# Quantised layer of an eight-stage transformer kernel: weight rounded on GpSimd in quarters, transforms placed in the gaps of the scale chain, products in groups

## What is computed

```python
def _compute_scale(t):
    return FP8_MAX / jnp.maximum(jnp.max(jnp.abs(t)), 1e-12)
def _quantize_fp8(t, scale):
    return jnp.clip(t * scale, -FP8_MAX, FP8_MAX).astype(jnp.float8_e4m3fn)
# third pair, feed-forward: one scale for all of layernorm(x), one for the weight
x_scale, w_scale = _compute_scale(x2), _compute_scale(weight)
out = jnp.matmul(_quantize_fp8(x2, x_scale).astype(f32), _quantize_fp8(weight.T, w_scale).T.astype(f32))
x = x + out * (1.0 / x_scale * (1.0 / w_scale))
# fourth pair, attention: correlation by Fourier transforms of x and of the context
corr = ifft(fft(q) * conj(fft(k))).real      # k and v are the context, so their transforms do not depend on x
```

## Time and profile before

| | |
|---|---|
| median of 3 runs | 1503.25 us (1502.2 to 1504.23) |
| profiled execution, its own time | 1506.02 us |
| its span (first to last instruction) | 1504.3 us |
| busy share PE / DVE / ACT / POOL | 92% / 72% / 51% / 48% |
| mean granted TensorE clock | 0.974 |
| the stage `quantised_ffn` in it | from 1195.05 us to 1235.78 us; the next stage's first matmul starts at 1236.90 us |

### The profile page before, as it was taken

One profiled execution on the slowest core, in us unless ns is written; L12 is line 12 of the kernel. 1 busy time (PEld: TensorE's weight loads), 2 busy tenths in 40 slices (PEclk: granted clock), 3 DMA queues, 4 the chain that ended last, 5 costly groups with the idle time before them and its releaser, 6 DMA issues. The chain is left out here.

```text
span 1504.3 us, 31394 instructions
## 1 busy us (share of the span) xinstructions
PE 1388.1 (92%) x11352; PEld 828.5 (55%) x11352; DVE 1076.6 (72%) x2125; ACT 762.6 (51%) x2476; POOL 723.0 (48%) x748
## 2 busy tenths in 40 slices
PE   5888599998999999888999999999999688889998
PEld 4776244445777777545555555655555235434444
DVE  7998555645666766667989888898877889965212
ACT  4777363222433433347766666666665457655111
POOL 4788552012434433856666666666665405734000
PEclk9999699999999999899999999999999899999999
DMA  7999572225999998757765556756534401646000
GB/s 187 191 174 175 127 182 41 55 39 107 171 180 198 166 153 133 131 134 172 152 146 112 117 114 109 141 112 117 106 73 80 131 3 28 132 84 112 22 7 28
DMA packets 524569, 174.62 MB, mean 116 GB/s; under 512 B 482576, under 2 KB 507600, under 8 KB 524416
## 3 DMA queue, kind: packets, MB, share of 16 engines
q1 hardware_dynamic: 524416, 172.62, 59.3%
HBM read 53.27 MB, written 2.10 MB: 37 GB/s over the span
## 5 line engine op out<-in xcount | busy, mean ns | idle before, releaser
L1887 POOL TENSOR_TENSOR a_q_ss<-a_q_ss,half 128x4 f32<-128x4 f32 x64 | 90.2, 1410 | 167.3 <-DVE a_q_ss L1796 83.8
L1709 ACT ACTIVATE a_probs<-a_masked,a_negmax 128x128 f32<-128x128 f32 x256 | 99.6, 390 | 101.4 <-DVE a_negmax L1767 101.4
L72 PE MATMUL bank<-a_wq_hi,xn_pair 128*128 128x512 f16 (+1 forms) x384 | 140.0, 365 | 8.7 <-DVE a_v_hl L1129 3.8
L1224 POOL TENSOR_TENSOR a_p_hl<-a_probs,a_p_hl 128x512 f16<-128x512 f32 x64 | 74.4, 1163 | 143.3 <-DVE a_p_hl L1145 143.3
L73 PE MATMUL bank<-a_wq_lo,xn_pair 128*128 128x512 f16 (+1 forms) x384 | 139.9, 364 | 0.0
L74 PE MATMUL bank<-a_wq_hi,xn_pair 128*128 128x512 f16 (+1 forms) x384 | 139.7, 364 | 0.0
L72 PE MATMUL bank<-a_wo_hi,a_o_hi 128*128 128x512 f16 x256 | 97.5, 381 | 4.4 <-DVE x_state L1783 3.5
L73 PE MATMUL bank<-a_wo_lo,a_o_hi 128*128 128x512 f16 x256 | 97.4, 380 | 0.0
L74 PE MATMUL bank<-a_wo_hi,a_o_lo 128*128 128x512 f16 x256 | 97.3, 380 | 0.0
L1902 POOL TENSOR_TENSOR a_normal<-a_probs,a_recip 128x512 f32<-128x512 f32 x64 | 90.3, 1410 | 5.0
L652 POOL TENSOR_TENSOR a_p_hl<-a_probs,a_p_hl 128x512 f16<-128x512 f32 x64 | 77.7, 1226 | 25.8 <-DVE a_p_hl L563 17.4
(11 more groups left out here) (472 smaller groups left out, 5017.2 us busy)
## 6 DMA issues: line engine op xcount, KB each, us to landing
a_no<-in_L_xattn_Wo SPq DMA_DIRECT2D x9, 1024.0 KB, 5.8
a_nq<-in_L_xattn_Wq SPq DMA_DIRECT2D x8, 1024.0 KB, 5.8
a_n_wq<-in_L_xattn_Wq SPq DMA_DIRECT2D x4, 768.0 KB, 6.2
a_n_wo<-in_L_xattn_Wo SPq DMA_DIRECT2D x4, 768.0 KB, 6.6
a_nk<-in_L_xattn_Wk SPq DMA_DIRECT2D x9, 256.0 KB, 3.2
a_nv<-in_L_xattn_Wv SPq DMA_DIRECT2D x9, 256.0 KB, 3.8
f_v_hat<-in_L_ffn_w SPq DMA_DIRECT2D x2, 1152.0 KB, 6.8
x_state<-in_x SPq DMA_DIRECT2D x8, 256.0 KB, 4.4
```

What stands on the lines that cost most here:

```text
L72: pe.matmul(out, lh, rh, start=start, stop=False)
L1224: pool.tensor_tensor(p_hl[s % PN][:, 1, t, :], probs[unit(s, t) % PROBS][:, :, :].rearrange("p h n -> p (h n)"), p_hl[s % PN][:, 0, t, :], ...
L1709: m = act.activation(probs[s % 2][:, h, :], src, ACT.Exp, bias=negmax[s % 2][:, h:h + 1], accum_out=total[s % 2][:, h:h + 1])
L1887: pool.tensor_tensor(r[:, :], r[:, :], K.half[:, 0:n], ALU.pow).then_inc(root_done.sem, 1)
```

## The change

- POOL takes over three of the four rounding steps of the weight (`round_weight`), in quarters of 128x512, by four instructions a quarter. DVE keeps the exponent bits (`exponents`), now per quarter, and no longer touches the whole weight.
- The first eight transforms stand between the transposes of the scale chain: one behind the first, two behind the second, one behind the third, four behind the fourth. The tables `spec` and `vspec` are loaded in the stage before, on SP behind the context, into buffers that live longer.
- The columns of the rows have eight buffers (`xq_t`), so ACT no longer waits for products; `tw` is filled three batches ahead.
- The products are done in groups: none before the transposes of batch 4, then 0 and 1; 2; 3 and 4; 5, 6 and 7. DVE's adds follow: 0 after rounding 5; 1 and 2 after 6; 3 after 7; the others among the statistics.

```diff
@@ wide_attention, SP
                     if s == TOTAL:
                         quant.load_context(sp, quant_in)
+                        for name, tile in (("spec", down.spec), ("vspec", down.vspec)):
+                            sp.dma_start(tile[:, :, :], tables[name]).then_inc(tables_in, 16)
                 sp.wait_ge(quant_in, 32)
+                sp.wait_ge(tables_in, 32)
@@ quantised_ffn
-    EARLY, FIRST = 12, 6
-    LATER = {i: list(range(EARLY + 2 * i, EARLY + 2 * i + 2)) if i < 4 else [EARLY + 4 + i] for i in range(B)}
+    AHEAD, RING, LEAD = 2, 3, 8
+    SPREAD = [[0], [1, 2], [3], [4, 5, 6, 7]]
...
+    PRODUCTS = {4: [0, 1], 5: [2], 6: [3, 4], 7: [5, 6, 7]}
+    ADDS = {5: [0], 6: [1, 2], 7: [3]}
...
-        xq_t, ident16 = [sb(f"xq_t{i}", [P, KT, P], BF16) for i in range(2)], sb("ident16", [P, P], BF16)
+        xq_t, ident16 = [sb(f"xq_t{i}", [P, KT, P], BF16) for i in range(B)], sb("ident16", [P, P], BF16)
@@ POOL
+                def round_weight(k):
+                    w, bits = Q.nw[:, k, :], Q.te[:, k, :].bitcast(F32)
+                    pool.wait_ge(w_bits, k + 1)
+                    pool.tensor_scalar(w, w, -Q.FP8_MAX, Q.FP8_MAX, ALU.max, ALU.min).then_inc(w_clipped, 1)
+                    pool.tensor_scalar(bits, bits, 2.0 ** -6, Q.MAGIC, ALU.max, ALU.mult).then_inc(w_magic, 1)
+                    pool.wait_ge(w_clipped, k + 1)
+                    pool.wait_ge(w_magic, k + 1)
+                    pool.tensor_tensor(w, w, bits, ALU.add).then_inc(w_sum, 1)
+                    pool.wait_ge(w_sum, k + 1)
+                    pool.tensor_tensor(wq[:, k, :], w, bits, ALU.subtract).then_inc(w_rounded, 1)
...
+                for k in range(KT):
+                    round_weight(k)
@@ DVE
+                def exponents(k):
+                    dve.wait_ge(w_scaled, k + 1)
+                    dve.tensor_scalar(Q.te[:, k, :], Q.nw[:, k, :].bitcast(I32), 0x7F800000, None, ALU.bitwise_and).then_inc(w_bits, 1)
...
+                for k in range(2):
+                    exponents(k)
                 widen(1)
+                exponents(2)
                 scale(1)
-                bits = Q.te.bitcast(F32)
-                dve.wait_ge(w_scaled, KT)
-                link(dve.tensor_scalar(Q.te, Q.nw.bitcast(I32), 0x7F800000, None, ALU.bitwise_and))
-                link(dve.tensor_scalar(bits, bits, 2.0 ** -6, Q.MAGIC, ALU.max, ALU.mult))
+                exponents(3)
                 round_fp8(0)
-                link(dve.scalar_tensor_tensor(Q.nw, Q.nw, -Q.FP8_MAX, bits, ALU.max, ALU.add))
-                dve.scalar_tensor_tensor(wq[:, :, :], Q.nw, Q.TOP, bits, ALU.min, ALU.subtract).then_inc(w_rounded, 1)
...
@@ PE
+                def product(b):
+                    pe.wait_ge(t_bank.freed(b), t_bank.n_drained(b))
...
+                    y_bank.wait_free(pe, b)
+                    for k in range(KT):
+                        if b == 0:
+                            pe.wait_ge(w_rounded, k + 1)
+                        m = pe.matmul(y_bank[b][:, :], xq_t[b][:, k, :], wq[:, k, :], start=(k == 0), stop=(k == KT - 1))
...
+                for b in batches:
+                    turned(b)
+                    beside(BESIDE[b])
+                    for ready in PRODUCTS.get(b, []):
+                        product(ready)
@@ ACT
+                spectra.copy(act, 0)
                 act.wait_ge(scale_done[0], 1)
                 for k in range(KT):
-                    act.activation(Q.nw[:, k, :], Q.nw[:, k, :], ACT.Copy, scale=Q.scale[:, 0:1]).then_inc(w_scaled, 1)
+                    scale_weight(k)
+                    if k < 3:
+                        spectra.copy(act, k + 1)
                 act.wait_ge(scale_done[1], 1)
...
-                    if b >= 2:
-                        act.wait_ge(y_bank.filled(b - 2), y_bank.n_filled(b - 2))
```

More of the change, by code:

```diff
@@ L2601, in quantised_ffn @@
         spread = K.bank[2:4]
-        w_scaled, w_rounded = K.sem("f2_w_scaled"), K.sem("f2_w_rounded")
+        w_scaled, w_bits, w_clipped, w_magic, w_sum, w_rounded = (
+            K.sem(f"f2_w_{n}") for n in ("scaled", "bits", "clipped", "magic", "sum", "rounded"))
         batches = list(range(B))
@@ L2682, in _ @@
                 link(dve.tensor_tensor(Q.out_by[:, :], Q.back[:, 0:1], Q.back[:, 1:2], ALU.mult))
-                for b in batches:
-                    if b:
-                        round_fp8(b)
-                    if b >= 2:
-                        add(b - 2)
+                for b in batches[1:]:
+                    round_fp8(b)
+                    for done in ADDS.get(b, []):
+                        add(done)
                 for b in range(AHEAD):
-                    K.take_stats(dve, b).then_inc(next_stats, 1)
-                add(B - 2)
+                    stats_ahead(b)
+                add(4)
                 for b in range(AHEAD):
-                    dve.wait_ge(next_stats, b + 1)
-                    dve.bn_aggr(Q.mv[:, b, :], K.stats[:, b, :]).then_inc(next_mean, 1)
-                add(B - 1)
+                    mean_ahead(b)
+                add(5)
+                add(6)
                 dve.wait_ge(next_root, 1)
@@ L2697, in _, with turned @@
                     dve.tensor_scalar(xn[:, b, :], K.x[:, b, :], Q.mv[:, b, 0:1], Q.rstd[:, b:b + 1], ALU.subtract, ALU.mult)
+                add(7)
             @block.tensor
             def _(pe):
[L2701 to L2712, removed]
+                def turned(b):
                     pe.wait_ge(q_done.sem, q_done.count(b))
@@ new lines, in beside @@
+                def beside(part):
+                    for u in part:
+                        spectra.multiply(pe, u)
+                pe.transpose(spread[0][0:1, 0:P], Q.big[:, 0:1], K.ident[:, :]).then_inc(in_row[0], 1)
+                beside(SPREAD[0])
+                pe.wait_ge(along_done[0], 1)
+                pe.transpose(spread[0][:, P:P + 1], along[:, 0, :], K.ident[0:1, 0:1]).then_inc(in_column[0], 1)
+                beside(SPREAD[1])
+                pe.wait_ge(largest_done, 1)
+                pe.transpose(spread[1][0:1, 0:P], Q.big[:, 1:2], K.ident[:, :]).then_inc(in_row[1], 1)
@@ L2731, in _ @@
+                beside(SPREAD[2])
+                pe.wait_ge(along_done[1], 1)
+                pe.transpose(spread[1][:, P:P + 1], along[:, 1, :], K.ident[0:1, 0:1]).then_inc(in_column[1], 1)
+                beside(SPREAD[3])
+                pe.wait_ge(const_done, 2)
+                for b in batches:
[3 more added lines that the diff above has]
+                        product(ready)
             @block.scalar
@@ L2738, in _, with scale_weight, columns @@
+                def scale_weight(k):
+                    act.activation(Q.nw[:, k, :], Q.nw[:, k, :], ACT.Copy, scale=Q.scale[:, 0:1]).then_inc(w_scaled, 1)
+                def columns(b):
+                    act.wait_ge(t_bank.filled(b), t_bank.n_filled(b))
+                    act.activation(xq_t[b][:, :, :], t_bank[b][:, :].bitcast(BF16)[:, 0:DIM].rearrange(
+                        "p (k t) -> p k t", k=KT), ACT.Copy).then_inc(t_bank.freed(b), 1)
+                spectra.copy(act, 0)
                 act.wait_ge(scale_done[0], 1)
@@ L2739, in _ @@
                 for k in range(KT):
-                    act.activation(Q.nw[:, k, :], Q.nw[:, k, :], ACT.Copy, scale=Q.scale[:, 0:1]).then_inc(w_scaled, 1)
+                    scale_weight(k)
+                    if k < 3:
+                        spectra.copy(act, k + 1)
                 act.wait_ge(scale_done[1], 1)
-                for b in range(2):
-                    scale(b)
-                for u in range(FIRST):
+                scale(0)
+                scale(1)
+                spectra.copy(act, 4)
@@ L2745, in _ @@
+                scale(2)
+                for u in range(5, LEAD):
                     spectra.copy(act, u)
                 for b in batches:
-                    act.wait_ge(t_bank.filled(b), t_bank.n_filled(b))
-                    if b >= 2:
-                        act.wait_ge(y_bank.filled(b - 2), y_bank.n_filled(b - 2))
-                    act.activation(xq_t[b % 2][:, :, :], t_bank[b][:, :].bitcast(BF16)[:, 0:DIM].rearrange(
-                        "p (k t) -> p k t", k=KT), ACT.Copy).then_inc(t_bank.freed(b), 1)
@@ L2752, in _ @@
-                    if b + 2 < B:
-                        scale(b + 2)
-                    for u in (LATER[b] if b else range(FIRST, EARLY + 2)):
+                    columns(b)
+                    if b + RING < B:
+                        scale(b + RING)
+                    for u in BESIDE[b]:
                         spectra.copy(act, u)
```

55 lines of the change are left out of this document (28 added, 27 removed).

## The result

Six runs of each kernel on one chip gave a median of 1511.61 us for the change (1507.95 to 1515.15) and 1503.24 us for the kernel before (1501.44 to 1505.07). The ratio is 1.0048, with a 95% interval of 1.0032 to 1.0064: slower by about half a per cent. The forecast had the side right (slower, 1506.2 us) and the size too small. 1511.61 lies 1.1 us above the range's high end of 1510.5; the ratio, applied to the 1503.25 us from which the forecast started, gives 1510.5, the high end itself.

The account below looks back on a forecast made before the run. PE and DVE were taken as two close bounds, with DVE's path setting the stage's end. Terms 0.9 - 4.5 - 1.65 + 7.8 + 0.85 - 0.5 = +2.9 us took the median from 1503.25 to 1506.2 us; range 1497.5 to 1510.5.

Parts of the forecast that it names:

- Rival A: Rounding on DVE and weight on POOL do not hinder each other: -5.5 us, 1497.8 us; chance 0.23.
- Item 1: Tables loaded early on SP's queue, behind the context: no effect on time.
- Item 2: Transforms in the scale chain's gaps at the stage's head delay the first rounding on DVE: +0.9 us.
- rival C: Transforms in the scale chain's gaps run at half clock, chain 1.4 us longer: 1507.6 us; chance 0.15.
- Item 3: The weight's two wide steps leave DVE: -4.5 us.
- Item 4: ACT's wait for products gone, ring three ahead, so DVE's stall at 1216.50 goes: -1.65 us.
- Item 5: POOL's sixteen weight instructions and DVE's roundings exclude each other, three quarters on rounds 0 to 2: +7.8 us.
- rival B: DVE keeps the port, POOL's weight ends late and product 0 waits: +6.4 us, 1509.7 us; chance 0.12.
- Item 6: Products in groups: add 0 on DVE waits, +0.85 us; adds fill the wait for POOL's root, -0.5 us.
- if product 0 waits for POOL: Sign at PE's first product that the forecast is wrong, pointing to rival B.
- if the first rounding starts after 1204.5: Sign on DVE after the scale chain that the forecast is wrong, pointing to rival C; forecast start 1203.3.
- the dear price: POOL's one-input steps cost 1.27 us instead of 0.61: 4.0 us more, 1510.2 us, behind the range's high end.

Follow-up runs that it names:

- e2: The changed kernel with products reading a stand-in that ACT fills and POOL's sixteen weight instructions left out; ratio 0.9968 to the kernel before, stage 38.13 us.
- e4: The changed kernel with all eight early transforms behind the scale chain instead of in its gaps; ratio 1.0055 to the kernel before, stage 47.07 us.
- e3: The changed kernel with the weight rounded on DVE as before, everything else of the change kept; ratio 1.0027 to the kernel before, stage 46.24 us.
- e11: The kernel before with eight buffers of turned rows, no ACT wait for products, rows scaled three batches ahead; ratio 0.9993, stage 40.07 us.
- e10: The kernel before with eight buffers of turned rows and without ACT's wait for products; ratio 1.0002, stage 41.71 us.
- e8: The changed kernel with each POOL tensor_scalar doing one operation, the other left out; one run, 1512.84 us, stage 47.40 us.
- e1: The changed kernel with products reading a stand-in that ACT fills, POOL's work still running but unawaited; ratio 1.0038 to the kernel before, stage 46.59 us.
- e13: The changed kernel with POOL's work unawaited and its two tensor_tensors a quarter left out; one run, 1502.34 us, stage 39.55 us.
- e5: The changed kernel with POOL doing only its two tensor_tensors a quarter, DVE making the constant, no clip; ratio 1.0036 to the kernel before, stage 45.59 us.

## Why the prediction came out as it did

*The side* was right, by the reason given: rounding and weight hinder each other, and that costs more than the wide steps had. Rival A (POOL hides) is what e2 imitates: stage -3.72 and ratio 0.9968, against -5.5 and 1497.8 forecast. The chip did not allow it.

*Item 1 (tables), 0:* right, SP's wait for PE is 5.2 before and after.

*Item 2 (scale chain), +0.9:* too small. The first rounding starts 8.90 us from the stage's start instead of 7.38, +1.5. Transform 0 took 1.91 us at the low clock where I had taken 0.85, so the first column transpose came 1.1 us later and not 0.25. The transforms of the second gap both ran at the low clock too (3.72 us), and the scale of x came 3.1 us later. This is rival C's mechanism, which I had at 0.15, but for the fourth transform, which ran at full clock. But e4 shows that it hardly mattered here: sooner by 2.8, the stage kept 0.9.

*Item 3 (weight off DVE), -4.5:* the two steps are gone from DVE and nothing stands in their place. What I did not see is that the wide steps were time in which PE worked off transforms; with those placed in the gaps, putting the steps back (e3) leaves PE idle for 5.00 us.

*Item 4 (ACT's wait), -1.65:* the wait is gone, and e11 gives 1.78 on the kernel before. The cause was half right: the lead of three does it, the buffers alone do nothing (e10).

**Item 5 (POOL), +7.8, is the term that was mis-sized most.** It had two errors, of opposite sign.

The first is the price of the tensor_scalar. I took 0.61 us from the CAST, "since it also reads one tensor", with ends of 0.61 and 1.27. It took 1.94 to 2.13, outside both ends; e8 shows 1.5 to 1.9 with one operation. The trace of before had no such instruction, and the kinship of two operations with one input each was no bound. So a quarter took 7.2 us instead of 4.9, the four ran over six roundings instead of three, and the last ended 33.3 us after the stage's start, where I had 20 to 26. This is how rival B's consequence came about: product 0 waited 2.05 us for the weight, worth 1.41 (e1). Its mechanism, DVE keeping the port, did not: DVE was stretched as well.

The second is how much a tensor_scalar of POOL holds DVE. I let every instruction exclude the other engine for its length less 0.14. For the tensor_tensor that is about right (1.0 us measured, 1.14 taken). The long tensor_scalar costs DVE only some 0.4 (2.3 us for the six that lay beside roundings in e13). The Trainium skill (SBUF — State Buffer, "Who interferes with whom") lets the engine that issues first hold the pair for its whole instruction; by that the tensor_scalars of 1.95 us would have cost more still. The trace agrees for the tensor_tensor and not for the tensor_scalar.

Together the six roundings took 9.3 us more than in e2 (8.46 of it in the stage's length), against my 7.8, because quarter 0's tensor_tensors lay on the roundings as well, so that seven of them met DVE there and not six. With the first error alone my own rule would have given 6 x 1.33 = 8.0 us more, so that 7.8 came as near as it did is in part luck: the second error took back most of the first. The Trainium skill (GPSIMD Engine Reference, "Elementwise — side-by-side cycle accounting") has 769 ns for 512 elements in a tight loop; the tensor_scalar here took two and a half times that.

*Item 6 (groups):* add 0 waits 0.97 us in e2, where 0.85 was forecast. In the change it waits 1.60, and all of that is the late weight: in e1, with the roundings as long, it does not wait. The wait for POOL's root is gone, as forecast.

*The sum:* +2.9 forecast, +6.15 in the stage. By e1 and e2 the missing 3.25 is 1.4 for the late weight, 0.7 for the contention (8.46 against 7.8) and 1.2 for the rest of the change (-3.72 against the -4.9 of the other items). Of this 1.2, item 2 is 0.6 and item 6 is 0.1; the last 0.4 or 0.5 I can't place. By median the change costs 8.4 us and by the ratio 7.2. I named it to be wrong "if product 0 waits for POOL" and "if the first rounding starts after 1204.5": the first happened; the second nearly (1203.95 on that scale). The range was too narrow because its high end took the dear price from a row that bounded nothing.

## What to carry to other kernels

An instruction kind that the trace does not hold has no bound from a kind that looks alike; time it alone in one run before half a stage is built on it, or leave the range wide. POOL's tensor_tensor beside a DVE chain on SBUF costs DVE most of its own length: 1.0 us for each on a quarter of the weight, where DVE takes 2.28 / 4 = 0.57 a quarter for a step of its own. So such work is worth moving only to where DVE is idle or, by the one row of e1, works from PSUM; that POOL is idle is not enough. And before work is pulled from a busy place into a gap, ask what will fill the place it leaves: in e3 PE stood still there, and its clock fell.

## What was not expected of the hardware

- POOL's tensor_scalar on 128x512 f32 takes 1.94 us with two operations ahead of all roundings, 1.92 to 2.36 over all runs, and 1.5 to 1.9 with one (e8), longer than its tensor_tensor with two inputs (1.26).
- It yet hardly hinders DVE: a step with two inputs took its plain 0.69 inside one of 1.97 us (e13), while beside a tensor_tensor it took 1.78.
- A DVE copy of 128 elements on one partition took 1.19 us in place of 0.21 beside a tensor_tensor of POOL (e5), and a DVE tensor_tensor on 128x1 took 1.03 in place of 0.16 (e4, at 1203.62): size alone does not protect. Yet two other instructions on 128x1 beside one kept their 0.16 and 0.15 (e5, at 1205.80 and 1206.00); what decides is not settled here.
- PE idle for 5.00 us was followed by a granted clock of 0.50 over the next 5 us although PE was busy for all of them (e3): two transforms took 3.73 us, against 1.88 in the kernel before (at 1207.70).
